# Two sums and a subtraction moved to GpSimd, accumulator banks swapped, and h's first turn moved inside the second tile's ff2

## The reference, cut to what matters

```
y  = LN(x)
y  = LN(y + causal_attention(y, y, y)) * g1 + beta1
y  = LN(y + attention(y, ctx, ctx)) * g2 + beta2
y  = LN(y + relu(y @ w1 + b1) @ w2 + b2) * g3 + beta3      # w1: 256x1024, w2: 1024x256
x1 = x + y
xq = fp4_blocks(LN(x1))                                    # blocks of 16, scale = max|.| / 6
h  = silu(xq @ fp4_blocks(w_gate).T) * (xq @ fp4_blocks(w_up).T)    # 704 wide
x2 = x1 + fp4_blocks(h) @ fp4_blocks(w_down).T
```

## Time and profile before

| | |
|---|---|
| median of 3 runs | 654.2 us (652.0 to 654.75) |
| profiled execution, its own time | 655.71 us |
| its span, first to last instruction | 653.9 us |
| PE busy | 574.1 us (88%) |
| DVE busy | 525.4 us (80%) |
| ACT busy | 382.2 us (58%) |
| POOL busy | 355.8 us (54%) |
| mean granted TensorE clock | 0.958 |
| HBM | 14.62 MB read, 4.19 MB written |

### The profile page before, as it was taken

The page is one execution under the profiler, slowest core; times in us unless marked ns, Lnnn a source line. Parts: engine busy times, 40 slices in busy tenths (PEclk is TensorE's granted clock), DMA queues, the critical chain, the costliest instruction groups (busy, mean ns, idle before and its releaser), DMA issues.

```text
span 653.9 us, 12396 instructions
## 1 busy us (share of the span) xinstructions
PE 574.1 (88%) x3989; PEld 540.5 (83%) x3989; DVE 525.4 (80%) x1300; ACT 382.2 (58%) x781; POOL 355.8 (54%) x450
## 2 busy tenths in 40 slices
PE   3776769998999999999999899999999898988665
PEld 2665759898989898998989898989899898978565
DVE  3788677898878888888879888888889878988663
ACT  3456365665738575666657574766666664746331
POOL 3555363575646555575557555655657554654521
PEclk9777889999999999999999999999999999999886
DMA  7600000010100101010101010010101010000000
GB/s 223 207 2 33 1 15 28 1 49 1 41 18 20 32 1 58 0 48 0 56 0 48 1 32 24 0 48 0 56 2 33 2 33 2 18 1 18 0 17 16
DMA packets 18742, 19.30 MB, mean 30 GB/s; under 512 B 1536, under 2 KB 18192, under 8 KB 18704
## 3 DMA queue, kind: packets, MB, share of 16 engines
q1 hardware_dynamic: 18704, 18.82, 9.3%
HBM read 14.62 MB, written 4.19 MB: 29 GB/s over the span
## 4 chain that ended last, share of the span: by engine, by line
PE 53%; DVE 25%; issue 9%; ACT 6%; POOL 3%; DMA 1%; SPq 1%; DVEq 0%; POOLq 0%; ACTq 0%
PE R L925 4%; PE R L927 4%; PE R L926 4%; PE O L973 4%; PE O L1040 3%; PE O L1038 3%; PE O L1039 3%; PE TR L811 3%; PE R L992 3%; DVE hs L1314 3%; PE R L994 3%; PE R L993 3%; PE R L811 3%; DVE hT_lo L1341 3%; DVE hqT_lo L1347 2%
## 5 line engine op out<-in xcount | busy, mean ns | idle before, releaser
L456 POOL TENSOR_TENSOR rs<-mv,neg_half 128x1 f32<-128x1 f32 (+1 forms) x112 | 69.6, 627 | 47.3 <-DVE mv L1261 45.7
L925 PE MATMUL R<-gu_hi,xqT_hi 128*128 128x352 f32 x256 | 87.2, 341 | 4.3 <-issue 3.3
L992 PE MATMUL R<-y2T_hi,w_hi 128*128 128x256 f32 x256 | 76.6, 299 | 9.2 <-DVE y2T_lo L1397 6.5
L926 PE MATMUL R<-gu_lo,xqT_hi 128*128 128x352 f32 x256 | 83.9, 328 | 0.0
L927 PE MATMUL R<-gu_hi,xqT_lo 128*128 128x352 f32 x256 | 83.8, 327 | 0.0
L462 POOL TENSOR_TENSOR hs<-hh,h_rec 128x704 f32<-128x704 f32 x32 | 44.6, 1393 | 69.2 <-DVE h_rec L1297 69.2
L677 ACT ACTIVATE hqT_hi<-R 128x768 fp32r<-128x768 f32 x32 | 26.0, 813 | 90.7 <-PE R L811 90.7
L1038 PE MATMUL O<-w_hi,hT_hi 128*128 128x256 f32 x256 | 73.7, 288 | 0.0
L994 PE MATMUL R<-y2T_hi,w_lo 128*128 128x256 f32 x256 | 72.7, 284 | 0.0
L993 PE MATMUL R<-y2T_lo,w_hi 128*128 128x256 f32 x256 | 72.6, 284 | 0.0
L1039 PE MATMUL O<-w_lo,hT_hi 128*128 128x256 f32 x256 | 72.4, 283 | 0.0
(11 more groups left out here) (153 smaller groups left out, 1827.7 us busy)
## 6 DMA issues: line engine op xcount, KB each, us to landing
x_in<-in_x SPq DMA_DIRECT2D x16, 256.0 KB, 2.8
x_res<-in_x SPq DMA_DIRECT2D x16, 256.0 KB, 2.9
out<-x SPq DMA_DIRECT2D x32, 128.0 KB, 1.7
ctx_rows<-in_ctx SPq DMA_DIRECT2D x16, 64.0 KB, 2.5
hT<-in_L_xattn_w SPq DMA_DIRECT2D x1, 1024.0 KB, 7.9
hh<-in_L_xattn_w SPq DMA_DIRECT2D x1, 768.0 KB, 8.4
wd_raw<-in_L_ffn_w_down SPq DMA_DIRECT2D x1, 704.0 KB, 9.5
w_raw<-in_L_ffn_w_gate SPq DMA_DIRECT2D x1, 640.0 KB, 4.6
```

The lines of the kernel that those rows point to most:

```text
L456: pool.tensor_tensor(rs[i][:, t0:t0 + len(ts)], mv[i][:, t0:t0 + len(ts), 1], neg_half[:, 0:len(ts)], ALU.pow).then_inc(ln_rstd[i], 1)
L925: mm(o, xh, gu_hi[:, c, m, cols], start=(c == 0), stop=False)
L926: mm(o, xh, gu_lo[:, c, m, cols], start=False, stop=False)
L992: mm(o, w1_hi[:, c, cols], y2T_hi[:, c, :], start=(c == 0), stop=False)
```

## The change

`x1_sum` of both tiles goes from VectorE to GpSimd, behind `gamma3` of the same tile. The last of the four `h_lower` pieces becomes `h_lower_last` on GpSimd, with its own semaphore. `values(t)` and `down(t)` use O[t]. The first two eighths of ff2's second tile stand before the turn of h's first tile, the rest behind it. `hT_lower` is split in `hT_lower` and `hT_stack`; for the first tile the former moves from the next slot's start to this slot's end, ahead of `ff_sum(1)`. On ScalarE `norm_x` goes behind the copy of `y2T_hi`. On VectorE the order of several pieces changes. The waits follow.

```diff
         FF2_CUT = 5 * FC // 8
+        FF2_TURN = FC // 4
...
+            def h_lower_last(b, h):
+                wait(pool, h_hi_set, b, h, F, 4, 4)
+                pool.tensor_tensor(hT_lo[:, 6:8, :], hT[:, 6:8, :], hT_hi[:, 6:8, :].bitcast(F32),
+                                   ALU.subtract).then_inc(h_lo_last, 1)
...
                 if f1:
                     gamma3(b, g, 0)
+                    x1_sum(b, g, 0)
...
                     gamma3(b, g, 1)
+                    x1_sum(b, g, 1)
                     unscale_x(b, g, 0)
...
                 if q:
                     scale_h(b, h, 0)
+                if f:
+                    h_lower_last(b, h)
...
+            def x1_sum(b, h, t):
+
+                wait(pool, y3_set, b, h, F, T, t + 1)
+                wait(pool, xb_set, b, h, F, T, t + 1)
+                wait(pool, x2_set, b, h, Q + 1, T, t + 1)
+                pool.tensor_tensor(x1[(h - F) % 2][:, t, :], z3[:, t, :], xb[:, t, :], ALU.add).then_inc(x1_set, 1)
...
-                if front:
-                    norm_x(b, h)
                 if f:
...
                                    ACT.Copy).then_inc(y2T_hi_set, 1)
+                if front:
+                    norm_x(b, h)
...
+                    wait(pe, z2_set, b, h, F, T, T)
+                else:
                     wait(pe, z3_set, b, h, F + 1, T, T)
-                else:
-                    wait(pe, z2_set, b, h, F, T, T)
...
-                    last = mm(O[1 - t][:, 0:D + 1], e, y0[:, key, :], start=(i == 0), stop=(i == len(lhs) - 1))
+                    last = mm(O[t][:, 0:D + 1], e, y0[:, key, :], start=(i == 0), stop=(i == len(lhs) - 1))
...
-                o = O[1 - t][:, 0:D]
+                o = O[t][:, 0:D]
...
                     cross_values(b, h)
+                if f:
+                    ff2(b, h, 1, range(FF2_TURN))
                 if q:
                     turn_hq(b, h, 0)
                 if front and h == 0:
                     turn_context(b)
                 if f:
-                    ff2(b, h, 1, range(FC))
+                    ff2(b, h, 1, range(FF2_TURN, FC))
...
+            def hT_stack(b, h, t):
+                wait(dve, hqT_hi_set, b, h, Q, T, t + 1)
+                base, w = TURNED, IW - P
...
                 if q1:
-                    hT_lower(b, g, 0)
+                    hT_stack(b, g, 0)
...
                 if f1:
-                    x1_sum(b, g, 0)
+                    z3_stats(b, g, 1)
                     x1_stats(b, g, 0)
+                    aggregate(3, b, g, F, 1)
                     aggregate(4, b, g, F, 0)
-                    z3_stats(b, g, 1)
-                    aggregate(3, b, g, F, 1)
+                if a:
+                    self_reciprocal(b, h, 1)
+                    self_sum(b, h, 1)
+                if f1:
                     x_norm(b, g, 0)
+                if q1:
+                    hT_lower(b, g, 1)
+                    hT_stack(b, g, 1)
+                if f1:
                     x_max(b, g, 0)
                     x_scale(b, g, 0)
                     x_reciprocal(b, g, 0)
                     shift(3, b, g, F, (1,))
-                if q1:
-                    hT_lower(b, g, 1)
-                if a:
-                    self_reciprocal(b, h, 1)
-                    self_sum(b, h, 1)
...
                     x_drop(b, g, 0)
-                    x1_sum(b, g, 1)
...
                     xT_lower(b, h, 0)
+                if q1:
+                    down_add(b, g, 1)
...
-                if f:
-                    h_lower(b, h, (3,))
-                if q1:
-                    down_add(b, g, 1)
...
                     h_product(b, h, 1, 1)
-                    h_lift(b, h, 0)
                 if a:
                     cross_max(b, h)
                 prepare(b, h, "cross")
                 if q:
+                    h_lift(b, h, 0)
                     h_drop(b, h, 0)
-                    h_max(b, h, 1)
                 if a:
                     cross_reciprocal(b, h)
                     cp_lower(b, h)
+                if q:
+                    h_max(b, h, 1)
+                    h_scale(b, h, 1)
+                    h_reciprocal(b, h, 1)
                 if f:
                     ff_sum(b, h, 0)
                 prepare(b, h, "late")
                 if a:
                     cross_sum(b, h)
-                if q:
-                    h_scale(b, h, 1)
-                    h_reciprocal(b, h, 1)
...
                     aggregate(3, b, h, F, 0)
+                if a:
+                    shift(2, b, h, A, (0, 1))
+                if q:
+                    hT_lower(b, h, 0)
+                if f:
                     ff_sum(b, h, 1)
                 if front:
                     shift(0, b, h + 1, 0, (0, 1))
-                if a:
-                    shift(2, b, h, A, (0, 1))
```

More of the change, by code:

```diff
@@ L226, in layer_program @@
         n2_turned, y2T_hi_set, y2T_lo_set = sem("n2_turned"), sem("y2T_hi_set"), sem("y2T_lo_set")
-        ff1_done, relu_set, h_hi_set, h_lo_set = sem("ff1_done"), sem("relu_set"), sem("h_hi_set"), sem("h_lo_set")
+        ff1_done, relu_set, h_hi_set, h_lo_set, h_lo_last = (sem(n) for n in (
+            "ff1_done", "relu_set", "h_hi_set", "h_lo_set", "h_lo_last"))
         ff2_done, z3_set = sem("ff2_done"), sem("z3_set")
@@ L1027, in ff2 @@
                     wait(pe, h_hi_set, b, h, F, 4, n)
-                    wait(pe, h_lo_set, b, h, F, 4, n)
+                    wait(pe, h_lo_set, b, h, F, 3, min(n, 3))
+                    if n == 4:
+                        wait(pe, h_lo_last, b, h, F, 1, 1)
                     if fs[0] == 0:
-                        wait(pe, x2_set, b, h, Q + 1, T, 1)
+                        wait(pe, x2_set, b, h, Q + 1, T, T)
                 else:
@@ L1050, in cross_values @@
                     wait_batch(pe, ctx_lo_set, b, 1, 1)
-                wait(pe, x2_set, b, h, Q + 1, T, T)
+                wait(pe, x2_set, b, h, Q + 1, T, 1)
                 for t in range(T):
@@ L1355, in down_add @@
                 store_wait(b, h, t)
-                v.tensor_tensor(x2[:, t, :], O[1 - t][:, 0:D], x1[(h - Q) % 2][:, t, :], ALU.add).then_inc(x2_set, 1)
+                v.tensor_tensor(x2[:, t, :], O[t][:, 0:D], x1[(h - Q) % 2][:, t, :], ALU.add).then_inc(x2_set, 1)
             def store_wait(b, h, t):
@@ L1363, in ff_sum @@
                 wait(dve, y2_set, b, h, F, T, t + 1)
+                wait(dve, x1_set, b, h, F + 1, T, t + 1)
                 v.tensor_tensor(z3[:, t, :], O[1][:, 0:D], y2[t][:], ALU.add).then_inc(z3_set, 1)
[L1366 to L1370, removed]
             def x1_stats(b, h, t):
@@ L1401, in self_reciprocal @@
                 wait(dve, pv_done, b, h, A, T, t + 1)
-                v.reciprocal(rsum1[:, t:t + 1], O[1 - t][:, D:D + 1]).then_inc(rsum1_set, 1)
+                v.reciprocal(rsum1[:, t:t + 1], O[t][:, D:D + 1]).then_inc(rsum1_set, 1)
             def self_sum(b, h, t):
@@ L1407, in self_sum @@
                 wait(dve, rsum1_set, b, h, A, T, t + 1)
-                v.scalar_tensor_tensor(z1[:, t, :], O[1 - t][:, 0:D], rsum1[:, t:t + 1],
+                v.scalar_tensor_tensor(z1[:, t, :], O[t][:, 0:D], rsum1[:, t:t + 1],
                                        y0[:, T * half + t, 0:D], ALU.mult, ALU.add).then_inc(z1_set, 1)
```

## The result

| | before | after |
|---|---|---|
| median, runs of one comparison | 654.48 us (652.0 to 655.92, 4 runs) | 671.56 us (669.01 to 673.18, 4 runs) |
| profiled execution, its own time | 655.71 | 669.01 |
| its span | 653.9 | 667.2 |

The ratio of the medians is 1.0249, 95% interval 1.0215 to 1.0284: the change makes the kernel slower. The forecast was 665 in a range of 647 to 673, with 0.65 for slower. The profiled execution is 13.3 us longer than before's (forecast 11.5). The profile speaks of these 13.3 us; the medians lie 17.1 apart (forecast some 10.5, from 654.5 to 665). So a difference of two spans can be off by a few us, and where it matters the medians stand beside it.

The account below looks back on a forecast made before the run. It took TensorE's matmuls plus its waits as the bound. 29.1 us lost (17.5 + 7.4 + 1.2 + 2 + 1) less 17.6 back gives +11.5 on 655.7, so 667.2; the median forecast was 665, range 647 to 673.

Parts of the forecast that it names:

- What would show it: Signs in the new profile: ff2's second tile, ff1(2), first values and scores waits as forecast, a pair about 72.5 us.
- three signs against it: A pair of 70 us or less, second-tile h_max finished before cpT's turn, or clock below 1.00 in full slots.
- Back: TensorE waits the change removes: values 8.1, scores 4.2, ce turn 4.0, y2T_hi 1.3, together 17.6 us.
- `scores` 4.2: Scores' waits for h's stacked tail: hT_lower(1) ahead of x_max to shift removes the 1.0 us kind, 4.2 us back.
- The `ce` term: TensorE's turn of ce: h_lift(0) behind cross_max gives back 4 of 6.1 us, bounds 0 and 6.1.
- First wait: ff2's second tile on TensorE waits for late ff_sum(0), 1.25 us in 14 slots: 17.5 us, bounds 0 and 21.
- Second wait: exp_diag late for ff1(2), with the delays behind it: 7.4 even slots, 1.2 odd, 2 gate_up, 1 drain.
- The first three terms: exp_diag late for ff1(2), 7.4 us in even and 1.2 in odd slots, and gate_up late, 2 us.
- The drain: Last slots, where TensorE has little work and the x chain is exposed: its later start costs about 1 us, 0 to 3.
- B: ScalarE's queue isn't late, relu or exp get through in the gap, so no exp_diag wait: 655 us, chance 0.16.
- C: ff_sum(0) is not late on TensorE's path, so the kernel is faster: 648 us, chance 0.16.
- D: New GpSimd sums hold up VectorE's x_lift or x_drop, 0.7 us in each of 14 slots: 675 us, chance 0.14.

Follow-up runs that it names:

- 1: The kernel after with h_max(1) before cp_lower and h_scale(1), h_reciprocal(1) behind cross_sum on VectorE, so ff_sum(0) runs early: 656.02 us, ratio 1.0022.
- number 2: The kernel after with x_max(0) to shift(3, 1) back ahead of hT_lower(1) and hT_stack(1) on VectorE: 652.42 us, ratio 0.9964.
- number 3: The kernel after with both VectorE orders put back (early ff_sum(0); x_max(0) to shift ahead of hT_lower(1)): 634.77 us, ratio 0.9697.
- number 4: The kernel before with only h_max(1), h_scale(1) and h_reciprocal(1) moved between cp_lower and ff_sum(0): 664.71 us, ratio 1.0163.
- number 5: The kernel before with only hT_lower(1), stack included, moved ahead of x_max(0) to shift(3, 1) on VectorE: 666.98 us, ratio 1.0192.
- number 7: The kernel before with only the accumulator banks swapped (values(t) and down(t) in O[t], waits to match): 649.76 us, ratio 0.9927.
- number 8: Two runs against number 3, giving GpSimd work back to VectorE: both x1_sum, 641.99 us; the last quarter of hT_lo, 638.13 us.
- number 9: number 3 with h_scale(1) and h_reciprocal(1) between ff_sum(0) and cross_sum on VectorE: 630.05 us, ratio 0.9639.

## Why the prediction was right, and where its size was luck

The mechanism was right: both new waits are where it put them, and each was shown twice, by taking it out of the kernel after (1, 2, 3) and by putting its cause alone into the kernel before (4, 5). By its own steps:

- **What would show it.** ff2's second tile waits 1.36 us in a full slot (forecast 1.24 to 1.25), `exp_diag` 1.07 in even ones (about 1.2), the first `values` waits for `ff_sum` nowhere, all `scores` wait 0.31, a pair lasts 72.97 (72.5), the clock is 1.00. None of the three signs against it came.
- **Back: 17.6 forecast, 21.3 measured** (before against number 3), of which 19.3 stand in the rows of waits of the kernel after: `values` 8.1 (8.1), `scores` 4.2 (4.2), `ce` 5.8 (4.0), `y2T_hi` 1.2 (1.3). The `ce` term was mis-sized. By the medians 20.2 came back, with an interval that holds 17.6, so the whole term isn't shown to be off. And these rows are no savings that add up: the banks alone brought 5.5 of their 8.1 (number 7), while the sums on GpSimd, costed at nothing, are worth 7.2 (number 8), since without them `scores` would wait for longer, and the quarter of `hT_lo`, also costed at nothing, is worth 3.4. The prediction put the 4.2 us down to the place of `hT_lower(1)`. That place does it in the kernel before (number 5), but with the sums gone from VectorE it isn't needed: in number 2, without it, the 4.2 us are kept. The amount was right, the cause only half.
- **First wait: 17.5 forecast; 21.0 less the 0.8 that number 3 also shows in one place = 20.2 us of idle time; 13.5 to 16.5 of span, 15.5 to 17.7 by the medians.** The walk through the queue held to 0.12 us. The span loses less than the idle time because TensorE's wait here makes others shorter: without it, `values` waits 2.6 us in odd slots. From ff2's first shift row (L1055) to the turn of h, start to start, number 3 takes 1.43 and 1.32 us less than number 2 in the two slots of a pair, and from there to the next `scores` 0.43 and 0.24 more.
- **Second wait: 7.4 + 1.2 + 2 + 1 = 11.6 forecast; 18.1 to 21.1 of span, 19.1 to 21.3 by the medians.** This is the mis-sized one. The first three terms, 10.6 us in six pairs, are 1.77 a pair; measured 2.28. The drain was put at 1 us with an upper bound of 3, and measured 6.9 (number 2 against after): the term that failed.
- **Net.** -21.3 + 13.5 + 21.1 = +13.3 (to rounding), forecast +11.5. That the total is near is partly luck: 3.7 us too little given back, and 34.6 lost where 29.1 were forecast. And the spans flatter it: by the medians the change costs 17.1 us where about 10.5 were forecast, and 671.6 lies 1.4 us inside the range's end.

The tail of the kernel after, TensorE's timeline in one of the last slots:

```profile
596.51 0.36 PE L1033 MATMUL O<-wd_hi,hqT_hi 128*128 128x256 f32 x1 [0.37 <-issue]
...
601.22 0.44 PE L829 MATMUL TR<-ident,xq 128*128 128x128 f32 x2 [1.04 <-POOL xq L594]
...
604.95 0.40 PE L943 MATMUL R<-gu_hi,xqT_hi 128*128 128x352 f32 x1 [1.86 <-issue]
```

and number 2, where the turn of xq waits for nothing:

```profile
582.91 0.35 PE L1033 MATMUL O<-wd_hi,hqT_hi 128*128 128x256 f32 x1 [0.46 <-issue]
...
589.24 0.40 PE L943 MATMUL R<-gu_hi,xqT_hi 128*128 128x352 f32 x1 [1.01 <-issue]
```

The turn of xq waits in three of the last slots, 2.8 us in all in the waits after and not at all in number 2; gate_up waits for 1.87, 1.86 and 1.72 us where it waits for 0.74, 1.01 and 0.98 in number 2, 2.7 us more: 5.5 in brackets. Start to start, from the down projection (L1033) to gate_up, the three slots take 8.44, 8.44 and 7.09 us after and 6.05, 6.33 and 5.37 in number 2, which makes 6.2 of the 6.9 us. The start of the x chain slipped by about the same time in these slots as in the full ones, but here nothing else of TensorE's list covers it.

The rivals. B (ScalarE not late) fell with the `exp_diag` row and number 5, C (`ff_sum(0)` not late) with the `ff_sum` row and number 4. D (the sums on GpSimd hold `x_lift` and `x_drop`) had its mechanism and not its effect. In number 2 VectorE's two pieces lie beside GpSimd's `gamma3` and `x1_sum`:

```profile
338.81 0.75 DVE L1347 SCALAR_TENSOR_TENSOR wd_raw<-xa,wd_raw 128x256 f32<-128x256 f32 x1
339.59 0.83 DVE L1352 SCALAR_TENSOR_TENSOR xa<-xa,wd_raw 128x256 f32<-128x256 f32 x1
```
```profile
338.55 0.73 POOL L577 TENSOR_TENSOR w_raw<-w_raw,g_row 128x256 f32<-128x256 f32 x1 [0.81 <-ACT w_raw L653]
339.35 0.79 POOL L584 TENSOR_TENSOR w_raw<-w_raw 128x256 f32<-128x256 f32 x1
```

0.75 and 0.83 us instead of 0.43 each (the second takes 0.42 in the kernel of number 8, with no sum beside it), about the 0.7 us that D named. Each of them ends 0.28 us after the GpSimd piece beside it, and these have nearly their usual length (0.73 and 0.79, where the shortest of either is 0.72). By the Trainium skill ("SBUF — State Buffer", "Who interferes with whom") the two engines exclude each other on a shared pair of ports; the trace agrees, and here it is VectorE that pays. But giving the sums back to VectorE costs 7.2 us in number 3, so there D is refuted as a loss. In the kernel after that edit wasn't tried. There the two pieces of the first tile take 0.64 and 0.85 us, some 0.6 more than alone, in a chain that TensorE waits for in the last slots, so part of the tail's 6.9 us can be D's; how much isn't shown.

`h_lower_last` took 1.27 us on GpSimd in this even slot and 1.46 in odd ones (forecast 1.6, bounds 0.94 to 1.88), and `x1_sum` 0.74 to 0.81 (0.8). `unscale_h(0)` stayed hidden as the prediction says: hq is ready at 364.98 and turned at 367.59.

```profile
360.04 1.27 POOL L497 TENSOR_TENSOR hT_lo<-hT,hT_hi 128x512 fp32r<-128x512 f32 x1
...
364.69 0.29 POOL L473 TENSOR_TENSOR hq<-ha,h_div 128x64 f32<-128x64 f32 x1
```

Open: 0.7 of the 6.9 us that the second wait costs in the tail, and D's share in that tail, why number 9 gave 4.7 us and not 2.4, and how the 21.3 us divide over the parts of the change that were not tried alone (`y2T_hi`, `h_lift(0)`, `self_sum(1)`, the split of `hT_lower(0)`).

## What to carry to other kernels

In an in-order queue the place of a piece counts more than the load: look for the engine's idle time before each handover, put work there whose input is ready and that somebody needs soon, and let a piece that frees a bank for another engine go before those that nobody waits for. Moving one piece ahead of another pays only if its own input is there; else it makes the other late for nothing. Walk the pipeline's last slots by themselves, since a delay that full slots hide in part is paid in full there.

## What the runs showed of the hardware

- Of the instructions of VectorE with two SBUF inputs that overlap a GpSimd product or sum in these traces, the one that starts second pays. VectorE's `x_lift`, started 0.26 us behind `gamma3`, takes 0.75 instead of 0.43 (above). Where VectorE's 128x512 subtraction starts first, it keeps its usual 0.68, against 1.72 in the earlier trace rows, and GpSimd's product behind it takes 1.06 instead of 0.78, in 14 slots alike (after, VectorE, then GpSimd):

```profile
348.09 0.68 DVE L1363 TENSOR_TENSOR hT_lo<-hT,hT_hi 128x512 fp32r<-128x512 f32 x1
```
```profile
348.31 1.06 POOL L480 TENSOR_TENSOR beta_row<-w_raw,g_row 128x256 f32<-128x256 f32 x1
349.33 0.78 POOL L480 TENSOR_TENSOR b_row<-w_raw,g_row 128x256 f32<-128x256 f32 x1
```

- TensorE's idle time in the trace is less than what a wait costs, since matmuls overlap: 1.07 us listed at ff1's third pair, 1.07 + 0.28 - 0.12 = 1.23 measured from `scores` to there, and 2.0 in the slot with the waits behind it (number 2).
